# Two down projections of a two-layer block as seven products, and the place at which a decay tile takes its bank

## The reference

```python
x = x + attention(layernorm(x))   # linear attention with decay, 4 heads of 128, chunks of 128 rows
x = x + ffn(layernorm(x))
# ffn, with xt = 2048 x 512, and Wg, Wu (4096 x 512), Wd (512 x 4096) given as 4-bit codes and scales:
gate, up = xt @ Wg.T, xt @ Wu.T
out = (gelu(gate) * up) @ Wd.T
```

## Time and profile before

| | us |
|---|---|
| median of 3 runs | 1144.14 |
| lowest, highest | 1144.07, 1144.46 |
| the profiled execution | 1143.82 |
| its span | 1141.8 |
| TensorE busy | 1136.0 |
| VectorE, GpSimd, ScalarE busy | 694.8, 535.3, 446.1 |

### The profile page before, as it was taken

The page is one execution under the profiler, slowest core; times in us unless marked ns, Lnnn a source line. Parts: engine busy times, 40 slices in busy tenths (PEclk is TensorE's granted clock), DMA queues, the critical chain, the costliest instruction groups (busy, mean ns, idle before and its releaser), DMA issues.

```text
span 1141.8 us, 19963 instructions
## 1 busy us (share of the span) xinstructions
PE 1136.0 (99%) x8014; PEld 787.4 (69%) x8014; DVE 694.8 (61%) x1284; ACT 446.1 (39%) x1037; POOL 535.3 (47%) x530
## 2 busy tenths in 40 slices
PE   9999999999999999999999999999999999999999
PEld 5666655565467777777777777777777777777776
DVE  7788656367777855665566556655665566555334
ACT  4433334253344434343434343434343434343332
POOL 3386535155883945363536363635362536253110
PEclk9999999999999999999999999999999999999999
DMA  8021011000101010101010101010101010100111
GB/s 303 3 76 46 29 38 38 10 10 2 56 19 38 20 37 20 38 19 38 20 37 20 38 19 38 20 38 19 38 20 37 18 38 22 34 17 16 38 38 65
DMA packets 22828, 41.97 MB, mean 37 GB/s; under 512 B 2704, under 2 KB 3024, under 8 KB 22736
## 3 DMA queue, kind: packets, MB, share of 16 engines
q1 hardware_dynamic: 22736, 40.70, 11.3%
HBM read 36.46 MB, written 4.23 MB: 36 GB/s over the span
## 4 chain that ended last, share of the span: by engine, by line
PE 96%; POOL 1%; DVE 1%; ACT 0%; issue 0%; DMA 0%; SPq 0%; DVEq 0%; ACTq 0%; POOLq 0%
PE ps L518 45%; PE ps L558 29%; PE ps L348 8%; PE ps L479 7%; PE ps L314 1%; PE ps L440 1%; PE ps L423 1%; PE ps L447 1%; PE ps L434 1%; PE ps L358 1%; PE ps L414 1%; DMA WR<-wqkv 0%; POOL bigA L1302 0%; DVE wf L1122 0%; POOL kn_s L1327 0%
## 5 line engine op out<-in xcount | busy, mean ns | idle before, releaser
L558 PE MATMUL ps<-WR,ihl_s 128*128 128x512 f16 x768 | 184.7, 379 | 0.0
L518 PE MATMUL ps<-XT,WR 128*128 128x256 f16 x1344 | 183.3, 273 | 0.0
L518 PE MATMUL ps<-REG,WR 128*128 128x256 f16 x1344 | 183.3, 273 | 0.0
L1139 DVE TENSOR_TENSOR load<-load,ps 128x256 f32<-128x256 f32 x168 | 70.7, 421 | 179.8 <-PE ps L518 101.3
L558 PE MATMUL ps<-WR,vv 128*128 128x512 f16 x708 | 171.4, 379 | 0.0
L518 PEld LDWEIGHTS ps<-REG,WR 128*128 128x128 f16 x1344 | 131.5, 98 | 39.1
L814 ACT COPY load<-ps 128x256 f32<-128x256 f32 x168 | 62.6, 372 | 245.1 <-PE ps L518 245.1
L1139 DVE TENSOR_TENSOR bigB<-bigB,ps 128x256 f32<-128x256 f32 x168 | 70.6, 420 | 124.3 <-ACT bigB L814 93.2
L518 PEld LDWEIGHTS ps<-XT,WR 128*128 128x128 f16 x1344 | 131.5, 98 | 15.4
L814 ACT COPY bigB<-ps 128x256 f32<-128x256 f32 x168 | 62.6, 373 | 172.0 <-PE ps L518 172.0
L558 PEld LDWEIGHTS ps<-WR,ihl_s 128*128 128x128 f16 x768 | 75.2, 98 | 66.5
(11 more groups left out here) (180 smaller groups left out, 1793.6 us busy)
## 6 DMA issues: line engine op xcount, KB each, us to landing
load<-codes SPq DMA_DIRECT2D x48, 256.0 KB
load<-scales SPq DMA_DIRECT2D x48, 256.0 KB
y<-X SPq DMA_DIRECT2D x15, 256.0 KB, 2.0
bigA<-cla SPq DMA_DIRECT2D x14, 256.0 KB, 3.0
X<-x SPq DMA_DIRECT2D x3, 1024.0 KB, 13.2
WR<-wqkv SPq DMA_DIRECT2D x2, 1024.0 KB, 9.6
X<-x SPq DMA_DIRECT2D x4, 256.0 KB, 3.9
WR<-wqkv SPq DMA_DIRECT2D x4, 256.0 KB, 4.3
```

The costliest lines, as they stand in the source:

```text
L518: mm = eng.matmul(half_bank(kind, name), w(wp, kt), x(xp, kt), start=(first and n == 0), stop=(n == 5), skip_group_check=True)
L558: mm = eng.matmul(PS[bank][:, :], ih[:, ip, 128 * tt:128 * tt + 128], buf[:, wp, 8 + j, :], start=(j == 0 and p == 0), stop=(j == end and ...
L1139: eng.tensor_tensor(c, c, half_bank(kind, end), ALU.add).then_inc(s_comb, 1)
```

## The change

Down projections n = 29 and 30 are computed as seven products of half-size blocks instead of 48 matmuls. The 512 rows are halved (first and last 256), the inner values of n are halved into even and odd tiles, and the output columns are taken as alternate runs of 128. Each product is 12 matmuls of 256 columns on two row tiles (`seven`). The products are spread over the down slots of pairs 60 and 61 (n = 29), 62 and 63 (n = 30): in the gate call of an even pair the first inner half of P1 and P2 and then the second, in its up call P5 and P6; in the gate call of an odd pair P3 and P7, in its up call P4 in two halves. P1, P6, P7, P4 add up in bank 6, P2 and then P5, P3 in bank 7, and VectorE adds the bank into the quarter of X1 that is complete after each (`into_rows`), seven times for an n. A product waits for the eviction after the one before it in the same bank.

The operands are sums of blocks. For the inner tiles (pairs 58 to 61) VectorE forms four sums of 256 columns (`operand_sums`) at the end of the pair; ScalarE and GpSimd split even part, odd part and sums into high and low f16 (`operands_high`, `sums_high`, `operands_low`) in the next pair. For the weights, chunk 47's sums are made once by GpSimd and ScalarE, in pairs 58 and 59, with the code that makes those of gate and up. For this the inner values are put in another order on the host, and the four down tiles of every group are addressed through `at(j)`.

In attention `decay_bank(T)` is split from `decay(T)`. Bank 1 of the two is taken ahead of the projection k(1,1), its matmuls stay behind it.

```diff
+SEVEN = (29, 30)
+SEVEN_PAIRS = tuple(m for n in SEVEN for m in (2 * n, 2 * n + 1))
+SUMMED = 47
+IN_TURN = ("P1", "P2", "P5", "P6", "P3", "P7", "P4")
 DEQUANTED = (0, 1, 4, 5, 8, 9)
...
+def seventh(n, name):
+
+    return 7 * (n - SEVEN[0]) + IN_TURN.index(name) + 1
+
+
+def operand(m, part):
+
+    return 3 * (m - SEVEN_PAIRS[0]) + {"e": 1, "o": 2, "T": 3}[part]
 
...
             return ihl_r[:, j] if n >= 3 and n % 2 else ihl_s[:, j]
+
+        def part_of(m, a, part):
+
+            first, count = {"e": (0, 1), "o": (1, 2), "T": (3, 4)}[part]
+            cols = slice(256 * (m % 2), 256 * (m % 2) + 256)
+            if m // 2 == SEVEN[0]:
+                return WR0[:, a, first:first + count, cols]
+            return ihl_s[:, 0:4, a, cols] if part == "T" else WR0[:, a, 8 + first:8 + first + count, cols]
+
+        def X1_of(n, half, odd):
+            rows_ = X1[:, 4 * (n % 4) + 2 * half:4 * (n % 4) + 2 * half + 2, :]
+            return rows_.rearrange("p t (u e n) -> p t u e n", u=2, e=2)[:, :, :, odd, :]
 
...
                 mm.then_inc(s_cum, 1)
 
+            def decay_bank(T):
+                bank_of["dec", T] = banks.take(pe, (s_dec, T + 1))
+
             def decay(T):
-                s = T % 2
-                bank = bank_of["dec", T] = banks.take(pe, (s_dec, T + 1))
+                s, bank = T % 2, bank_of["dec", T]
                 pe.wait_ge(s_setup, 7)
...
                 pe.wait_ge(s_snap, pair_base(kind, m, 3) + 1)
                 product("P6", comb(0), sums(1))
-                down(n, tt, (0, 1))
+                if n in SEVEN:
+                    seven_first(kind, m, n)
+                else:
+                    down(n, tt, (0, 1))
                 pe.wait_ge(s_snap, pair_base(kind, m, 3) + 2)
                 product("P7", comb(1), sums(2))
-                down(n, tt, (3, 2))
+                if n in SEVEN:
+                    seven_second(kind, m, n)
+                else:
+                    down(n, tt, (3, 2))
                 pe.wait_ge(s_snap, pair_base(kind, m, 3) + 3)
                 product("P4", left(2, o0), sums(3))
                 pe.wait_ge(s_comb, pair_base(kind, m, 3) + COMBINED["C22"])
                 product("P3", comb(2), toks(2, 256))
...
+            def seven(n, name, tts=(0, 1), us=(0, 1)):
+
+                bank = 6 if name in ("P1", "P6", "P7", "P4") else 7
+                last = {"P1": "P4", "P2": "P3", "P5": "P2", "P3": "P5", "P6": "P1", "P7": "P6", "P4": "P7"}[name]
+                if name in ("P1", "P2"):
+                    if n > SEVEN[0]:
+                        pe.wait_ge(s_out7, seventh(n - 1, last))
+                    else:
+                        for sm, value in banks.freed[bank]:
+                            pe.wait_ge(sm, value)
+                else:
+                    pe.wait_ge(s_out7, seventh(n, last))
+                pe.wait_ge(s_whi, whi_count(SUMMED, 1))
+                pe.wait_ge(s_wlo, wlo_count(SUMMED, 1))
+                if name in ("P5", "P6", "P3", "P7"):
+                    pe.wait_ge(s_wsum, pair_count(SUMMED))
+                part = {"P1": "e", "P2": "o", "P3": "o"}.get(name, "T")
+                at = {"P3": 1, "P6": 1, "P7": 2, "P4": 3}.get(name, 0)
+                pe.wait_ge(s_olo, operand(2 * n + us[-1], part))
+
+                def weight(wp, u):
+                    if name in ("P5", "P6", "P7", "P3"):
+                        side = {"P6": 0, "P7": 1, "P3": 2}
+                        return S1[wp][:, u, :] if name == "P5" else wide("down", 7, wp, side[name])[:, u, :]
+                    row = WR1[:, wp, (8 if name == "P1" else 10) + u, :].rearrange("p (v e n) -> p v e n", v=2, e=2)
+                    return row[:, :, 1 if name == "P4" else 0, :]
+
+                for tt in tts:
+                    for u in us:
+                        for ip, wp in ((0, 0), (0, 1), (1, 0)):
+                            x = part_of(2 * n + u, ip, part)[:, at, 128 * tt:128 * tt + 128]
+                            mm = eng.matmul(PS[bank][:, 256 * tt:256 * tt + 256], x, weight(wp, u),
+                                            start=(name in ("P1", "P2", "P5") and tt == u == ip == wp == 0),
+                                            stop=(u == 1 and ip == 1), skip_group_check=True)
+                if tts[-1] and us[-1]:
+                    mm.then_inc(s_seven, 1)
+
+            def seven_first(kind, m, n):
+                if m % 2 == 0 and kind == "gate":
+                    seven(n, "P1", us=(0,))
+                    seven(n, "P2", us=(0,))
+                elif m % 2 == 0:
+                    seven(n, "P5")
+                elif kind == "gate":
+                    seven(n, "P3")
+                else:
+                    seven(n, "P4", (0,))
+
+            def seven_second(kind, m, n):
+                if m % 2 == 0 and kind == "gate":
+                    seven(n, "P1", us=(1,))
+                    seven(n, "P2", us=(1,))
+                elif m % 2 == 0:
+                    seven(n, "P6")
+                elif kind == "gate":
+                    seven(n, "P7")
+                else:
+                    seven(n, "P4", (1,))
+
             def down(n, tt, js=(0, 1, 2, 3)):
 
...
                     ih = slot(4 * n + j)
-                    weights(6 * g + 4 + j // 2, j % 2)
+                    weights(6 * g + 4 + j % 2, j // 2)
                     pe.wait_ge(*ilo(4 * n + j))
                     for p, (ip, wp) in enumerate(((0, 0), (0, 1), (1, 0))):
-                        mm = eng.matmul(PS[bank][:, :], ih[:, ip, 128 * tt:128 * tt + 128], buf[:, wp, 8 + j, :],
+                        mm = eng.matmul(PS[bank][:, :], ih[:, ip, 128 * tt:128 * tt + 128], buf[:, wp, at(j), :],
...
             qkv("k", 1, 0)
             qkv("q", 1, 1, gates_sum)
+            decay_bank(0)
             decay(0)
             for T in range(NT):
                 i, fill = T - APART, fills(T)
                 head(T)
+                if T == 0:
+                    decay_bank(1)
                 for f in fill:
                     qkv(*f)
                     if f == fill[0] and T == 0:
...
-            banks.ring = [6, 2, 3, 7]
+            banks.freed[6], banks.freed[7] = [(s_out7, seventh(SEVEN[-1], "P4"))], [(s_out7, seventh(SEVEN[-1], "P3"))]
+            banks.ring = [7, 2, 3, 6]
             banks.turn = 0
...
+            def operands_high(m):
+
+                ac.wait_ge(s_inter, whole(2 * m))
+                ac.wait_ge(s_prod, pair_base("up", 55, 7) + 7)
+                if m // 2 > SEVEN[0]:
+                    ac.wait_ge(s_dn, 4 * SEVEN[0])
+                eng.copy(part_of(m, 0, "e")[:, 0, :], fw[:, 0, 0:256]).then_inc(s_ohi, 1)
+                eng.copy(part_of(m, 0, "o"), two(fw[:, 1, :])).then_inc(s_ohi, 1)
+
+            def sums_high(m):
+                ac.wait_ge(s_dsum, 4 * (m - SEVEN_PAIRS[0]) + 4)
+                eng.copy(part_of(m, 0, "T"), tsum).then_inc(s_ohi, 1)
...
+            def into_rows(n, name):
+
+                half, odd = {"P1": (0, 0), "P2": (0, 0), "P5": (1, 1), "P6": (1, 0), "P3": (1, 0), "P7": (1, 1),
+                             "P4": (0, 1)}[name]
+                bank = 6 if name in ("P1", "P6", "P7", "P4") else 7
+                block_ = X1_of(n, half, odd)
+                dv.wait_ge(s_seven, seventh(n, name))
+                earlier = {"P2": "P1", "P3": "P6", "P7": "P5"}.get(name)
+                if earlier:
+                    dv.wait_ge(s_out7, seventh(n, earlier))
+                eng.scalar_tensor_tensor(block_, PS[bank][:, :].rearrange("p (t u n) -> p t u n", t=2, u=2),
+                                         1.0 / (WS * IS), block_, ALU.mult, ALU.add).then_inc(s_out7, 1)
+
+            def operand_sums(m):
+                e, o, at = fw[:, 0, :], fw[:, 1, :], 4 * (m - SEVEN_PAIRS[0])
+                if m > SEVEN_PAIRS[0]:
+                    dv.wait_ge(s_olo, operand(m - 1, "T"))
+                dv.wait_ge(s_inter, whole(2 * m))
+                eng.tensor_tensor(tsum[:, 0, :], e[:, 256:512], e[:, 0:256], ALU.subtract).then_inc(s_dsum, 1)
+                eng.tensor_tensor(tsum[:, 2, :], o[:, 256:512], e[:, 256:512], ALU.subtract).then_inc(s_dsum, 1)
+                dv.wait_ge(s_dsum, at + 1)
+                eng.tensor_tensor(tsum[:, 1, :], o[:, 256:512], tsum[:, 0, :], ALU.subtract).then_inc(s_dsum, 1)
+                dv.wait_ge(s_dsum, at + 3)
+                eng.tensor_tensor(tsum[:, 3, :], o[:, 0:256], tsum[:, 1, :], ALU.subtract).then_inc(s_dsum, 1)
 
             def dq_bits(k):
...
+            def rows_of_second(m):
+
+                n = m // 2 - 1
+                if n not in SEVEN:
+                    gather(n, 2 * m % 4 + 1)
...
                 if m > 8:
-                    inter_low(oo - 2)
-                    inter_low(ee - 2)
-                    gather((m - 1) // 2 - 1, 2 * (m - 1) % 4 + 1)
+                    rows_of_second(m - 1)
...
                 combine("gate", m, "C12")
-                gather(n, 2 * m % 4)
```

(62 more changed lines are left out.)

44 lines of the change are left out of this document (33 added, 11 removed).

## The result

The kernel after took 1146.37 us in the median of 22 runs (1144.81 to 1147.95), the kernel before beside it 1144.09 us (22 runs, 1143.71 to 1145.22): a ratio of 1.0018, 95% interval [1.0012, 1.0024]. The forecast was 1143.7, range 1142.0 to 1145.1. It is outside, on the slow side; the change costs 2.3 us.

What follows compares the result with a forecast made beforehand. TensorE, busy 1136.0 of 1141.8 us, was taken as the bound; -2.38 + 1.9 + 0.2 - 0.1 = -0.4 us gave 1143.7, with an 8-in-10 range of 1142.0 to 1145.1.

Steps and rivals of the forecast that it cites:

- part 2: Early bank for the second decay in attention: the 0.92 us wait moves from L414 to L440, gain 0.1 us.
- R2: Rival on the early bank: TensorE keeps the whole 0.92 us, time 1142.9; chance 0.08 alone.
- part 1: Seven products for blocks 29 and 30 on TensorE: 1.19 us less a block, 2.38 for two, before added waits.
- (a): P2 of block 29, pair 60: TensorE waits for VectorE's eviction behind four sums, 1.9 us, ends 0.4 and 2.3.
- R1: Rival: no collision of VectorE's sums with GpSimd, wait at P2 only 0.4 us, time 1142.2; chance 0.15.
- (b): Up calls of pairs 61 and 63: P7 and P4 late behind ScalarE's snapshots, 0.2 us in all (0 to 0.5).
- (c): Evictions between products of one bank, at P5 and the first half of P4: slack 0.5 us, cost 0.
- R3: Rival: evictions into split rows slower, 1.1 us each, +0.8, time 1144.9; decides from 0.94 us an eviction; chance 0.08.
- (d): Operand chain: the low part of pair 59's sums is ready some 1 us before P5 of pair 60, cost 0.
- (e): Rest of the added work: chunk 47's sums, casts, evictions, new order of down weights, output rows; cost 0 each.

Runs made afterwards that it cites:

- e2_bank: The kernel before with only the second decay's bank taken early, against the kernel before: 1147.25 us, ratio 1.0025.
- e5_hold: Seven products without the early bank, GpSimd's low parts held until VectorE's four sums are done, against the kernel before: 1141.86 us, ratio 0.9983.

## Why the prediction was wrong

The step that failed is part 2, "I take 0.1, for somewhat fewer collisions with GpSimd", with its ends 0 and 0.92 on the side of a gain only; the runs show a loss of 2.93 in its place. That the wait moves from L414 to L440 was right, and R2 fell. What was wrong is the step from "VectorE is busy 10.71 of 10.85 us" to the conclusion that a small shift there costs nothing: the key scale "0.15 us sooner" was counted as a length. It is a phase. In the order of turns of VectorE and GpSimd it decides which operation meets which, and the two that met, L1266 and the pair L1290, stand ahead of the weighted scores. Alone the bank measures +2.93 us (e2_bank), +1.8 of it at the full clock. A full engine ahead of the new wait was a reason to give that step a bound on the loss side: one collision or two like those of the earlier trace rows would have put it at +0.85 or +1.7. The 0.15 was too small as well: GpSimd's small operations for the keys start 0.27 us sooner (5.01 us behind the weighted scores of tile 0, against 5.28), the scale L1515 0.64. The Trainium skill's rule on turns ("SBUF — State Buffer", "SBUF: two separate sides"), which the prediction used for part 1, speaks of just this; the trace agrees (L1266 takes 1.26 us behind the start of a GpSimd operation, 0.42 without). The prediction gave only a part of it, operations with two SBUF inputs, and did not apply it to part 2.

The second error is a term that was missing: the granted clock. The prediction took 1.00 as given. Behind the idle stretches of 0.70 and 1.88 us it fell in 15 of 22 runs, +1.5 us in the profiled one.

Part 1 held step by step. 109.2 ns a matmul, -2.38: right. (a) 1.9 forecast, 1.70 in the trace; its least end, 0.41, was 0.38 in e5_hold. R1 fell, since the collision came. (b) 0.2 forecast, 0 found: ScalarE's copy in the up call of pair 61 ends at 1101.98 and P7 starts at 1102.06, 0.08 behind it, where the forecast had put the 0.14 of a release by VectorE. (c) 0, right: the two evictions are done at 1086.4 (L1233), P5's products follow at 1086.99 without a wait; R3 needed 0.94 an eviction, they take 1.48 the pair. (d) 0, right: the low part is out at 1085.5. (e) nothing shows. The part alone gave -0.97 where these terms say -0.3 forecast and -0.68 traced; the rest is within what the start of the span varies.

## What to carry to other kernels

When a bank or buffer is freed earlier for an engine that next waits on a full queue, the wait moves, and the work it triggers moves too: ask what a shift of some tenths of a us makes its neighbours meet, and give the term a loss side with a collision for each pair of operations that may meet (two here, 1.80 us), and the clock on top. Put the operation that TensorE waits for ahead of the new vector work, not behind it: that one move was worth 1.3 to 1.9 us here (-0.97 without it, -2.29 and -2.85 with it) at no cost. Where a gap of TensorE can't be closed, its length alone is not its price, for the clock may fall behind it.
